# DLRM tower on one core: batch 1's one-hot rows compared in one run of 512 columns in place of three rows of 172

## The reference, cut to what matters

```
e = stack([tbl_f[ids[:, f]] for f in 26 fields])            # 2048 samples x 26 x 128
combined = concat([e, dense_x])                             # 2048 x 27 x 128
z = einsum('bfd,bgd->bfg', combined, combined)[:, triu]     # 351 pair products a sample
h = relu(concat([z, dense_x]) @ W_top1 + b_top1)            # 479 -> 512
h = relu(h @ W_top2 + b_top2)                               # -> 256
y = h @ W_top3                                              # -> 1
```

## Time and profile before

| | |
|---|---|
| runs, median (lowest to highest) | 398.76 us (397.82 to 400.59) |
| the profiled execution's own time | 394.82 us |
| its span on the core | 393.0 us |
| TensorE granted clock, mean | 0.965 of full |
| busy: TensorE matmul / VectorE / ScalarE / GpSimd | 344.2 / 273.1 / 212.4 / 275.1 us |
| compares of line 683 (batch 0) / line 689 (batches 1 to 3) | 56 / 216 |
| gathers of line 366 / line 372 | 272 / 8 |

### The profile page before, as it was taken

One profiled execution on the slowest core, in us unless ns is written; L12 is line 12 of the kernel. 1 busy time (PEld: TensorE's weight loads), 2 busy tenths in 40 slices (PEclk: granted clock), 3 DMA queues, 4 the chain that ended last, 5 costly groups with the idle time before them and its releaser, 6 DMA issues. The chain is left out here.

```text
span 393.0 us, 8127 instructions
## 1 busy us (share of the span) xinstructions
PE 344.2 (88%) x3279; PEld 254.7 (65%) x3279; DVE 273.1 (69%) x476; ACT 212.4 (54%) x359; POOL 275.1 (70%) x288
## 2 busy tenths in 40 slices
PE   4997896858998899988999799997999699989886
PEld 3665684747766476657777476575778355578785
DVE  6996899598997829499897919588996214142350
ACT  4563472674537446394637337392735646676642
POOL 7888777777777777777777777777777777776000
PEclk9998998979999999999999999998999799989999
DMA  7997242424243332524243332523312222221000
GB/s 188 256 265 186 55 110 70 106 55 103 60 110 82 79 77 53 135 55 96 70 106 81 78 80 55 133 58 81 82 48 57 53 56 53 55 55 49 2 2 0
DMA packets 24179, 33.35 MB, mean 85 GB/s; under 512 B 6527, under 2 KB 17538, under 8 KB 24144
## 3 DMA queue, kind: packets, MB, share of 16 engines
q0 software_dynamic: 8960, 18.37, 17.9%
q1 hardware_dynamic: 15184, 14.48, 15.7%
HBM read 32.82 MB, written 0.01 MB: 84 GB/s over the span
## 5 line engine op out<-in xcount | busy, mean ns | idle before, releaser
L366 POOL DMA_INDIRECT gat<-in_tbl,idx x272 | 265.2, 975 | 83.1 <-issue 82.8
L689 DVE TENSOR_SCALAR ring<-idb,rowid 125x516 fp32r<-125x516 int32 x216 | 147.0, 742 | 4.7 <-PE prod L427 3.4
L425 PE MATMUL prod<-ring,tab_hi 125*128 125x512 f32 x264 | 111.8, 424 | 10.3 <-DVE ring L689 7.3
L697 DVE COPY z<-gram 32x216 f32<-32x216 f32 x128 | 49.2, 384 | 94.9 <-PE gram L453 72.1
L427 PE MATMUL prod<-ring,tab_lo 125*128 125x512 f32 x264 | 106.8, 405 | 0.0
L585 ACT COPY ct<-front 128x512 f32<-128x512 f32 (+2 forms) x80 | 72.5, 957 | 4.5 <-PE front L399 4.0
L453 PEld LDWEIGHTS gram<-ct 128*64 128x64 f32 x2048 | 61.6, 138 | 14.9 <-issue 7.5
L425 PEld LDWEIGHTS prod<-ring,tab_hi 125*128 125x128 f32 x264 | 51.6, 195 | 29.8 <-DVE ring L689 14.0
L453 PE MATMUL gram<-ct 128*64 128x54 f32 x2048 | 64.6, 223 | 4.5 <-ACT ct L585 4.4
L427 PEld LDWEIGHTS prod<-ring,tab_lo 125*128 125x128 f32 x264 | 51.6, 195 | 9.9
L593 ACT COPY z<-gram 32x216 f32<-32x216 f32 x128 | 42.2, 329 | 19.1 <-PE gram L453 14.9
(11 more groups left out here) (72 smaller groups left out, 212.2 us busy)
## 6 DMA issues: line engine op xcount, KB each, us to landing
idb<-in_ids_t SPq DMA_DIRECT2D x27, 258.0 KB, 4.0
gat<-in_tbl,idx POOLq DMA_INDIRECT x272, 2.5
oh<-in_tbl SPq DMA_DIRECT2D x3, 448.0 KB
oh<-in_dense_t SPq DMA_DIRECT2D x4, 256.0 KB, 3.9
gat<-in_tbl SPq DMA_DIRECT2D x2, 448.0 KB
h<-in_tbl SPq DMA_DIRECT2D x2, 448.0 KB
w1z<-in_w SPq DMA_DIRECT2D x1, 702.0 KB
w2s<-in_w SPq DMA_DIRECT2D x1, 512.0 KB
```

The costliest lines, as they stand in the source:

```text
L366: nc.gpsimd.indirect_dma_start(out=gat[:, t % GS, i, :], out_offset=None, in_=tables[GATHERED[i]][:, :], in_offset=bass.IndirectOffsetOnAx ...
L425: nc.tensor.matmul(prod[:, :], tab_hi[0:OH_P, m, k, :], ring[0:OH_P, k, 0:SB], start=(k == 0), stop=False)
L689: nc.vector.tensor_scalar(ring[0:OH_P, k, :], idb[0:OH_P, n % IDB, :, 0:IW], rowid[0:OH_P, k:k + 1], None, ALU.is_equal).then_inc(built, 1)
L697: ins = nc.vector.tensor_copy(z1[QUAD * j:QUAD * (j + 1), c * CG:(c + 1) * CG, :], gram_bank(GC * t + c)[QUAD * j:QUAD * (j + 1), :, NF * ...
```

## The change

Batch 1's ids are loaded as one run of 512 columns into the same buffers, and each of its 72 compares reads that run and writes 512 columns of the slot. Batches 2 and 3 stay as they were, and batch 0 too. Products, order, waits and semaphores are the same.

```
+        def ids_run(n):
+            return idb[:, n % IDB, :, :].rearrange("p r c -> p (r c)")[:, 0:SB]
...
-                src = ids_t[m:m + 1, b * IR * IW:(b + 1) * IR * IW].rearrange("a (r c) -> a r c", r=IR)
-                sp.dma_start(idb[:, n % IDB, :, 0:IW], src.to_broadcast([P, IR, IW])).then_inc(idb_in[n % IDB], 16)
+                src = ids_t[m:m + 1, b * IR * IW:(b + 1) * IR * IW]
+                if b == 1:
+                    sp.dma_start(ids_run(n), src[:, 0:SB].to_broadcast([P, SB])).then_inc(idb_in[n % IDB], 16)
+                else:
+                    sp.dma_start(idb[:, n % IDB, :, 0:IW], src.rearrange("a (r c) -> a r c", r=IR).to_broadcast([P, IR, IW])
+                                 ).then_inc(idb_in[n % IDB], 16)
...
-                nc.vector.tensor_scalar(ring[0:OH_P, k, :], idb[0:OH_P, n % IDB, :, 0:IW], rowid[0:OH_P, k:k + 1], None,
-                                        ALU.is_equal).then_inc(built, 1)
+                if b == 1:
+                    nc.vector.tensor_scalar(ring[0:OH_P, k, 0:SB], ids_run(n)[0:OH_P, :], rowid[0:OH_P, k:k + 1], None,
+                                            ALU.is_equal).then_inc(built, 1)
+                else:
+                    nc.vector.tensor_scalar(ring[0:OH_P, k, :], idb[0:OH_P, n % IDB, :, 0:IW], rowid[0:OH_P, k:k + 1], None,
+                                            ALU.is_equal).then_inc(built, 1)
```

## The result

The changed kernel took 400.06 us (median of 20 runs, 395.61 to 404.62) against 397.55 us for the kernel before (median of 20, 392.48 to 401.31). The ratio is 1.0088, 95% interval 1.0053 to 1.0123: 0.9% or 3.5 us slower, by the medians 2.5 us. Forecast were +2.5 us. Every ratio here leaves out the runs more than 1.5% above the fastest of their own kernel, so it can differ from the ratio of the medians, which is 1.0063 here.

A forecast was written before the change was run, and what follows sets the result against it. TensorE was taken as the busiest engine, gated at tile 3's last fill by GpSimd's never-pausing gathers. Terms 2.0 - 0.3 + 0.8 = +2.5 us on the 398.76 us median gave 401.3 us; 8-in-10 range 397.0 to 406.5.

The forecast's parts named there:

- Compares: Batch 1's 72 compares on VectorE go from 742 ns to about 475 ns, saving about 17 us of VectorE time.
- Of all the savings at most 1.0 us is left: Before tile 3's last fill, TensorE gets early but GpSimd's gathers stop it, so at most 1.0 us is gained.
- The delay of GpSimd: Quick compares lengthen gathers: 3.0 us before tile 3's last fill, its own range 1.5 to 5.8; TensorE 2.0 us later there.
- The ten gathers taken as the price: Ten gathers beside compares alone, 4.83 to 40.87 us: excess 0 to 0.34 us, 0.16 each, times 19 gathers gives 3.0.
- No gather beside compares alone goes past the 1.28 at 21.39: Argument against charging batch 0's whole gather excess to its compares: the longest gather beside compares alone takes 1.28 us.
- An estimate of half a compare a gather: From the shared-port rule: a gather waits 0.24 us on average, so 18 gathers give 4.3 us in place of 3.0.
- The margin of 1.0 us: At tile 3's last fill, the last gather lands at 108.2 us and TensorE starts on it at 109.19.
- the clock term: A half-clock stretch after TensorE's waits around tile 3's last fill: +0.8 us, ends 0 and 1.7.
- The -0.3: At batch 1's last products, quicker last compares let tile 3's G come about 0.3 us sooner.
- Nothing gives it back: After tile 3's last fill the lateness stays to the end, as no later step hangs on its own clock.
- Rival B: Batch 0's whole gather excess is the compares': GpSimd delay 8.6 us, kernel +9.0 us, 407.8 us; chance 0.16.
- Rivals A and C: A: GpSimd undisturbed, kernel faster, 397.5 us, chance 0.14. C: compare no quicker, nothing moves, 398.8 us, chance 0.06.

The follow-up runs named there:

- e5: Changed kernel with batch 1's compare as three rows of 86 (258 columns) in place of one run of 512; 396.74 us, ratio 1.0015 to the kernel before.
- e8: Kernel before with the quick one-run compare in batch 3, batch 1 left as it was; 397.59 us, ratio 1.0051.
- e6: Changed kernel without tile 3's two extra gathers and their transposes; 398.95 us, ratio 1.0023 to the kernel before.
- e12: Kernel before with four small GpSimd memsets ahead of the gathers of tiles 1, 2 and 3 each, on a 659 to 660 us chip; ratio 0.9958.

## Why the prediction was right

- **Compares: right.** 478 ns median against the 475 taken, VectorE 16.8 us less busy against 17.
- **"Of all the savings at most 1.0 us is left": right.** The changed kernel waits for gathers at T3 of tile 2 and at T3 and T4 of tile 3, as was said. T2 of tile 2 was one more (4.33 us), and T2 of tile 3, also named, waits for ScalarE in this profile (1.68 us at 105.16). e5, which keeps the savings and drops the delay, isn't faster.
- **The delay of GpSimd: right in kind, mis-sized.** 3.0 us were forecast at tile 3's T4 for 64 compares, 0.047 us each. Measured were 5.3 us, 0.083 each, near the forecast's own upper bound of 5.8, and another 1.1 us came from batch 0, which two executions of the same code give (24 x (1.295 - 1.243) less 0.1). The ten gathers taken as the price had at most 0.34 us excess. The gather at 64.52 has 1.9: a gather can be kept out over several compares in turn. The trace of the kernel before already had such a one. "No gather beside compares alone goes past the 1.28 at 21.39" is a wrong reading, as these lines of GpSimd and VectorE show:

```profile
17.09 2.07 POOL L366 DMA_INDIRECT gat<-in_tbl,idx  x1 [0.30 <-issue]
```

```profile
15.80 3.25 DVE L683 TENSOR_SCALAR ring<-zt,rowid 125x512 fp32r<-125x512 f32 x8
18.96 1.21 DVE L673 TENSOR_TENSOR tab_lo<-oh,tab_hi 125x1024 fp32r<-125x1024 f32 x1
```

  By itself that gather would have ended at 18.03, but it was still open at 18.96, when the subtraction began, with only compares beside it till then. As an eleventh beside the ten it makes the price 0.25 us a gather and, with 18 gathers, 4.4 us in place of 3.0. The page "SBUF — State Buffer" of the Trainium skill, Who interferes with whom, says that the second of the two fully blocks until the first finishes. An estimate of half a compare a gather from it gave 4.3 us. The trace agrees with the blocking: the gather of 64.52 ends 0.1 us behind the train. But its 1.9 us are the time of nearly five compares started 0.40 us apart, so it waited for more than the first one.
- **The margin of 1.0 us: right for its profile, and not far off in another.** GpSimd's excess in batch 0 was 7.5 us in that profile and 8.6 to 11.8 in the others on such chips, with the same code there. That delay makes TensorE late as well. In e8, the kernel before as far as this step, the last gather starts at 108.97 and T4 at 111.98, a margin of 0.5 us with the same 2.5 us of landing.
- **T4 to G: the clock term mis-sized.** Forecast -0.3 + 0.8, measured +1.4. The half-clock stretch fell behind T4, at 114.9, and from the start of its first product to that of its last O(1,7) took 5.2 us in place of 3.6: +1.6, near the forecast's upper end of 1.7. The -0.3 came in the main: from its first product to G O(1,8) takes 3.9 us (121.42 to 125.31) in place of 4.1 (114.29 to 118.40). TensorE's wait in front of it, 0.88 us, is the same in both kernels. Before, the profile gives it to ScalarE's copy of the product bank, and behind the change to VectorE. But the first compares of O(1,8) start at 116.67, and that copy ends at 121.17:

```profile
114.29 0.47 PE L425 MATMUL prod<-ring,tab_hi 125*128 125x512 f32 x1 [0.88 <-ACT oh_last L564]
```

```profile
120.58 0.59 ACT L572 COPY oh_last<-prod 128x512 f32<-128x512 f32 x1 [4.37 <-PE prod L435]
```

- **"Nothing gives it back": right.** The 2.6 us that came back at 308 us are the clocks of two executions and not the change.

That the sum came out this close is in part luck. The two terms that were mis-sized, the delay (5.3 us for 3.0) and the clock (1.6 for 0.8), were both too small, and the two profiles are 6.9 us apart at G and 4.2 at the end, where the medians of the runs are 2.5 apart and the ratio gives 3.5. The profiled execution before had the smallest delay of GpSimd in batch 0 of the six on such chips and took 394.82 us, less than the median: against e8's G, 121.15, the changed kernel's is 4.2 us late and not 6.9. Rival B was near in its mechanism; the measured delay lies between the forecast's 3.0 and its 8.6 us. Rivals A and C are out.

## What to carry to other kernels

An engine that never pauses has no margin but the distance to its consumers: before a neighbour is made quicker, list for each consumer how far its last input lands ahead of it, and read whether the quicker form lengthens the busy engine's instructions. Here 17 us saved on VectorE bought nothing, and 5.5 us lost on GpSimd cost most of what they were. A price taken from a few overlaps can be too low where operations will run in trains; take every overlap in the trace, the worst too. And before two profiles are compared step by step, count both from a step behind the part that varies by itself.

## What the runs showed that I had not expected

- One gather was held for 1.9 us beside ten compares started 0.4 us apart, while others beside such compares had 0 to 0.3 us. In e6 it is so again: a train of ten starts at 65.87, a gather 1.30 us later at 67.17, as here, and it has the same 1.9 us of excess. So where in a train a gather starts seems to matter. The gathers' excess in batch 0 varies by 4 us between executions of the same code (7.5 to 11.8).
- A compare of 258 columns in three rows and one of 512 in one run take the same 476 and 478 ns; of these two only the second disturbs the gathers.
- The kernel before takes 397.4 us on some chips and 659 to 660 on others. There TensorE stands idle before some of its small pair products, 0.9 us on average and 2.6 at most in e12, and the profile names nothing that it waits for.
